# Bounds of the counting stage as 16-bit words without assertions, and in-degrees by one product per tile, in a four-layer graph network on one core

## The reference

```
x = layernorm(x + L0(x))   # attention, 4 heads: segment softmax of q[dst]*k[src], then a product, residual, norm
x = layernorm(x + L1(x))   # graph attention with loops, then a two-layer perceptron
x = layernorm(x + L2(x))   # h = x + segment_sum(relu(x[src]), dst); two dense layers; twice
x = layernorm(x + L3(x))   # graph convolution, then graph attention

def _gcn_conv(x, W, b, src, dst, n):      # first half of L3; src, dst with loops added
    xw = x @ W
    deg = jax.ops.segment_sum(jnp.ones(src.shape[0], x.dtype), dst, num_segments=n)
    dinv = jnp.where(deg > 0, jax.lax.rsqrt(deg), 0.0)
    norm = dinv[src] * dinv[dst]
    agg = jax.ops.segment_sum(xw[src] * norm[:, None], dst, num_segments=n)
    return agg + b
```

## Time and profile before

| | us |
|---|---|
| median of 3 runs | 3560.65 |
| lowest and highest | 3559.94 and 3570.57 |
| the profiled execution | 3559.3 |
| its span, first to last instruction | 3557.6 |
| PE busy | 3373.1 (95%) |
| DVE busy | 2598.0 (73%) |
| ACT busy | 2041.0 (57%) |

### The profile page before, as it was taken

The page is one execution under the profiler, slowest core; times in us unless marked ns, Lnnn a source line. Parts: engine busy times, 40 slices in busy tenths (PEclk is TensorE's granted clock), DMA queues, the critical chain, the costliest instruction groups (busy, mean ns, idle before and its releaser), DMA issues. The chain is left out here.

```text
span 3557.6 us, 67839 instructions
## 1 busy us (share of the span) xinstructions
PE 3373.1 (95%) x25864; PEld 2550.8 (72%) x25865; DVE 2598.0 (73%) x4774; ACT 2041.0 (57%) x3740; POOL 623.3 (18%) x602
## 2 busy tenths in 40 slices
PE   5999998999999999997999999999899999999999
PEld 3555555666676776766777777777688888878887
DVE  7888886666666666666999999999589443236665
ACT  2555556666666666665999899999311111115554
POOL 1000000111111111111235236666100100000000
PEclk9999999999999999998999999999999999999999
DMA  2555465233333333345333523333556555554341
GB/s 71 213 201 202 197 218 192 94 100 103 102 113 99 99 99 99 99 131 163 112 115 117 190 91 124 116 120 112 202 217 220 192 211 191 219 204 144 129 150 57
DMA packets 178028, 518.21 MB, mean 146 GB/s; under 512 B 54865, under 2 KB 140790, under 8 KB 144342
## 3 DMA queue, kind: packets, MB, share of 16 engines
q1 hardware_dynamic: 174822, 509.73, 41.2%
q10 hardware_dynamic: 1904, 3.81, 0.3%
q0 software_dynamic: 1024, 0.82, 0.1%
HBM read 353.04 MB, written 161.12 MB: 145 GB/s over the span
## 5 line engine op out<-in xcount | busy, mean ns | idle before, releaser
L1159 ACT ACTIVATE a_sm<-a_p_t 128x1024 f32<-128x1024 f32 (+1 forms) x800 | 669.6, 837 | 384.0 <-PE a_p_t L1095 378.2
L1095 PE MATMUL a_p_t<-ident,a_sm 128*128 128x128 f32 x5000 | 701.5, 280 | 35.4 <-ACT a_sm L1159 21.8
L1153 ACT ACTIVATE a_sm<-a_sm,a_negm 128x1024 f32<-128x1024 f32 (+2 forms) x600 | 702.8, 1171 | 49.8 <-DVE a_negm L1216 49.5
L1109 PE MATMUL a_p_o<-a_sm,a_v 128*64 128x128 f32 x10000 | 699.3, 278 | 19.0 <-ACT a_sumT L1166 17.7
L1095 PEld LDWEIGHTS a_p_t<-ident,a_sm 128*128 128x128 f32 x5000 | 559.1, 142 | 212.2 <-issue 193.0
L1109 PEld LDWEIGHTS a_p_o<-a_sm,a_v 128*64 128x64 f32 x10000 | 554.8, 137 | 196.6 <-issue 108.1
L1245 DVE CUSTOM_DVE_ANT_0 a_sm<-a_p_s,sh_rows 128x400 f32<-128x400 f32 x790 | 421.8, 571 | 345.6 <-PE a_p_s L1079 313.5
L1079 PE MATMUL a_p_s<-sh_wide,sh_q 64*128 64x400 f32 x1580 | 392.4, 550 | 12.0 <-DVE a_twice L1308 6.6
L1276 DVE CUSTOM_DVE_ANT_0 a_sm<-a_sm,sh_rows 128x3125 f32<-128x3125 f32 x100 | 348.5, 3485 | 1.3 <-issue 0.3
L1266 DVE SCALAR_TENSOR_TENSOR a_sm<-sh_wide,sh_al 128x3125 f32<-128x3125 f32 x100 | 346.9, 3469 | 3.5 <-PE a_p_o L1109 1.5
L693 ACT ACTIVATE sh_wide<-p_g 128x400 f32<-128x400 f32 x200 | 149.1, 901 | 246.5 <-PE p_g L608 246.5
(11 more groups left out here) (318 smaller groups left out, 4814.0 us busy)
## 6 DMA issues: line engine op xcount, KB each, us to landing
sh_rows<-d_full SPq DMA_DIRECT2D x67, 1600.0 KB, 7.0
sh_ct<-d_ct SPq DMA_DIRECT2D x50, 1600.0 KB, 6.8
d_ct<-sh_wide SPq DMA_DIRECT2D x25, 1600.0 KB, 5.3
d_full<-sh_rows SPq DMA_DIRECT2D x25, 1600.0 KB, 5.6
t_third<-d_ct SPq DMA_DIRECT2D x25, 1600.0 KB, 6.7
d_logs<-sh_rows SPq DMA_DIRECT2D x23, 1664.0 KB, 6.8
sh_rows<-d_logs SPq DMA_DIRECT2D x23, 1664.0 KB
t_mask<-d_full SPq DMA_DIRECT2D x8, 1600.0 KB, 6.8
```

The lines of the kernel that those rows point to most:

```text
L1095: m = nc.tensor.transpose(p_t[u % 2][:, i * P:(i + 1) * P], sm[buf][:, a * P:(a + 1) * P], ident[:, :])
L1109: m = nc.tensor.matmul(p_o[r:r + HD, 0:P], v[:, a, (p * heads + h) * HD:(p * heads + h + 1) * HD], sm[buf][:, a * P:(a + 1) * P], start=a ...
L1153: nc.scalar.activation(sm[buf][:, c], sm[buf][:, c], ACT.Exp, bias=negm[:, buf:buf + 1], accum_out=parts[:, buf, e:e + 1]).then_inc(s_prob, 1)
L1159: nc.scalar.activation(sm[buf][:, a_row[u] * P:a_row[u + 1] * P], p_t[u % 2][:, 0:turns[u] * P], ACT.Copy).then_inc(s_copy, 1)
```

## The change

`meta` becomes unsigned 16-bit. Both loads of it lose the run-time check of their bounds. The degree of a tile becomes one product: DVE adds `rest * real` into `by_low` after the reduction, and `s_by_low` counts two steps per tile.

```
-        meta = sb("meta", [1, NT, QPT * (2 + QUAD)], I32)
+        meta = sb("meta", [1, NT, QPT * (2 + QUAD)], U16)
...
                     _, said = nc.values_load_multi_w_load_instructions(
-                        meta[0:1, bass.ds(j, 1), :].rearrange("p n k -> p (n k)"), engines=[dve.engine], min_val=0, max_val=1 << 18)
+                        meta[0:1, bass.ds(j, 1), :].rearrange("p n k -> p (n k)"), engines=[dve.engine], min_val=0, max_val=(1 << 16) - 1, skip_runtime_bounds_check_because="loaded as unsigned 16-bit words")
...
                     _, said = nc.values_load_multi_w_load_instructions(
-                        meta[0:1, bass.ds(j, 1), 0:2 * QPT].rearrange("p n k -> p (n k)"), engines=[pe.engine], min_val=0, max_val=1 << 18)
+                        meta[0:1, bass.ds(j, 1), 0:2 * QPT].rearrange("p n k -> p (n k)"), engines=[pe.engine], min_val=0, max_val=(1 << 16) - 1, skip_runtime_bounds_check_because="loaded as unsigned 16-bit words")
...
-        pe.wait_ge(self.s_by_low, j + 1)
-        rest = self.ct[j % 3][:, (NT - 1) * P:NPAD].bitcast(FP32)
-        self.nc.tensor.matmul(self.p_deg[:, j:j + 1], rest, self.real[:, :], start=True, stop=False)
-        self.nc.tensor.matmul(self.p_deg[:, j:j + 1], self.by_low[j % 2][:, :], self.ones[:, :], start=False, stop=True).then_inc(self.s_deg_sum, 1)
+        pe.wait_ge(self.s_by_low, 2 * j + 2)
+        self.nc.tensor.matmul(self.p_deg[:, j:j + 1], self.by_low[j % 2][:, :], self.ones[:, :], start=True, stop=True).then_inc(self.s_deg_sum, 1)
...
-        self.nc.vector.tensor_reduce(self.by_low[j % 2][:, :], counts, AX.X, ALU.add).then_inc(self.s_by_low, 1)
+        rest = self.ct[j % 3][:, (NT - 1) * P:NPAD].bitcast(FP32)
+        by_low = self.by_low[j % 2][:, :]
+        self.nc.vector.tensor_reduce(by_low, counts, AX.X, ALU.add).then_inc(self.s_by_low, 1)
+        dve.wait_ge(self.s_by_low, 2 * j + 1)
+        self.nc.vector.scalar_tensor_tensor(by_low, rest, self.real[:, :], by_low, ALU.mult, ALU.add).then_inc(self.s_by_low, 1)
```

More of the change, by code:

```diff
@@ L10 @@
 I16 = mybir.dt.int16
+U16 = mybir.dt.uint16
 ALU = mybir.AluOpType
```

## The result

| | before | after |
|---|---|---|
| median of 4 runs each, lowest to highest (us) | 3563.13 (3559.94 to 3570.57) | 3524.54 (3521.93 to 3527.24) |
| ratio, 95% interval | | 0.9891 (0.9875 to 0.9906) |
| profiled execution, span | 3559.3, 3557.6 | 3527.2, 3525.5 |

The kernel became 1.1% faster, 38.6 us between the medians. The forecast was 1.5% (52 us, 3508), and the slow end of its range 3522. Lines of the counting stage have moved by one (537 is now 538, 545 is 546).

A forecast was written before the change was run, and what follows sets the result against it. DVE's sequencer bound the counting stage, with PE 0.6 us per tile behind; PE filled the last stage. Savings of 3.8, 3, 40 and 5.3 us made -52: 3508 us on the median's footing, range 3499 to 3522.

The forecast's parts named there:

- the price of the load: Counting stage, DVE's load of twelve table words per tile: stays 0.86 us with 16-bit words, at most twice that.
- The rest of the reckoning for DVE: Counting stage: DVE's 2.57 us gap before each tile's first key goes, leaving DVE 17.36 us per tile.
- DVE stays the bound: Rival, counting stage: dear 16-bit load or short sequencer lead leaves half the gap; period 18.6, 3521 us; chance 0.13.
- The assertions: Counting stage, DVE's sequencer: twelve pairs of register operation and assertion per tile go, worth 3.3 us (2.5 to 3.8).
- PE's floor: Counting stage: once DVE no longer starves it, PE binds at 18.0 us per tile.
- The rival of 18.4: Counting stage: PE also waits for ScalarE, so its floor is higher, period 18.4; 3517 us; chance 0.12.
- Terms of the stage: Counting stage savings: first tile -3.8 us, tiles 1 and 2 -3, tiles 3 to 24 -40.
- Part 2: Last stage's 25 sums: one degree product fewer each saves 5.5 us, less 0.2 in the first tile: -5.3.
- the margin: Last stage: DVE's fused operation stays hidden from PE, with 0.2 us left before the degree load, 0.1 before `t_h`.
- The dear fused operation: Rival, last stage: at 0.916 us PE waits for it every sum, turning -5.3 into +5; 3518 us; chance 0.04.
- Slower than before: Rival, counting stage: the 16-bit load takes over 4.2 us; 3600 us at 0.5 per word; chance 0.02.
- Transfers at nothing: Counting stage: transfers' share rises from 0.50 to 0.55 with the shorter tile; nothing charged.

The follow-up runs named there:

- e6: Changed kernel with PE loading all twelve words instead of four: PE's load 3.24 us instead of 0.99, period 18.70 us per tile instead of 18.67.
- e9: Changed kernel with DVE's load split into two of six 16-bit words, PE loading all twelve: 3546.45 us, ratio 0.9929 to the kernel before.
- e2: Changed kernel with the assertions kept on the 16-bit words: 3609.27 us, ratio 1.0128 to the kernel before.
- e1: Changed kernel with 32-bit words again, still without assertions, the number of earlier rounds masked: 3512.42 us, ratio 0.9858 to the kernel before.
- e10: e1 with the counting stage's stores of counts and logarithms cut to 128 columns per tile: period 18.10 us per tile.
- e11: e9 with the counting stage's stores of counts and logarithms cut to 128 columns per tile: period 18.13 us per tile instead of 20.23.
- e3: Kernel before with the new degree alone: 3560.44 us, ratio 0.9997 to the kernel before.
- e5: Changed kernel with a second, unread fused operation per degree: first degree to last 203.94 us instead of 199.15.
- e12: Changed kernel with the counting stage's stores of counts and logarithms cut to 128 columns per tile: period 18.59 us per tile instead of 18.67.
- e4: Changed kernel with each 16-bit word in a four-byte cell of its own: load 2.903 us, period 18.68 us per tile.
- e7: Changed kernel with signed 16-bit words, the number of earlier rounds masked: load 2.904 us, period 18.82 us per tile.

## Why the prediction was wrong

- **The failed step is the price of the load**: "I take 0.86: twelve words take 0.857 and four 0.333, about 0.066 each, which looks like a price per word, not per byte". Per word was right, on both engines (e6, e9). But two counts of one kind of word can't tell a price per word from one per 32-bit word. A 16-bit word costs 2.71 / 12 = 0.23 at an idle queue against 0.07, over three times as much, and the load of twelve takes 2.90 in the median. The upper bound, twice 0.86, was below that too; it was a guess without a row under it.
- **The rest of the reckoning for DVE held.** With 2.90 in place of 0.86 the same sum gives a gap of 2.57 - 3.3 + 2.04 = 1.31 and a period of 17.36 + 1.31 = 18.67. Measured: 1.34 and 18.67. So the price of the load is not one error among several in the loop, but the one that kept the bound at DVE.
- The Trainium skill, "Runtime: NRT & Kernel Launch", section "Instruction fetch mechanics", gives some 200 ns per register for such loads, of registers from HBM. I had set it aside because 32-bit words disagree (0.07). For 16-bit words the trace has 0.23 to 0.24, close to that figure, and the period it led to, 18.4, stood nearer to the 18.67 than my forecast. The nearness may be chance: the page speaks of another memory and says nothing of width. But it was a price for the same kind of instruction, and it should have set the upper bound of a form that no row showed.
- **The rival "DVE stays the bound"** came true with its mechanism (the 16-bit load is dear, about half the gap remains) and nearly its sizes: 18.6 and 3521, measured 18.67 and 3524.5. It had 0.13 of the chances, and the range ended with it, 2.5 us below the measured median.
- **The assertions**: 3.3 per tile forecast; by the periods of e2 and the changed kernel, which differ in them alone, 22.09 - 18.67 = 3.42. In e1, where nothing takes their place, DVE's gap is off the path and PE binds.
- **PE's floor**: 18.0 forecast, 18.11 in e1, 18.10 and 18.13 in e10 and e11. The rival of 18.4 is refuted.
- **Terms of the stage**: first tile -3.8 forecast, -1.2 measured (first product at 43.38 instead of 44.62; e1 -3.1); tiles 1 and 2 -3 forecast, -1.3 measured with tile 0 (e1 -1.9); tiles 3 to 24 -40 forecast, -26.4 measured (e1 -37.3). So of the 17.9 us missing in the stage, 13.4 are the narrow word, all of them back in e1, and 4.5 are missing in e1 too: 2.4 of them are the floor, 0.11 on 22 tiles, and what made the rest, mostly in the first three tiles, was not looked into.
- **Part 2**: -5.3 forecast; from the first degree to the last -5.3 in the changed kernel, -5.0 in e1 (199.47) and -3.9 in e3. The exact match is partly luck: one of the sums before took 8.67 where the others took 8.2. The steady gain is 0.21 per sum, as forecast. The fused operation was 0.34 in the forecast and is 0.352; the margin is as reckoned (e5). The dear fused operation (0.916) is refuted.
- **Slower than before** needed 4.2 us for the load. At 2.9 it kept 1.3 of distance; e2 shows what the same load does with the assertions beside it, 1.3% slower.
- **Transfers at nothing**: wrong in principle, though it cost little here. At shares of 0.13 and 0.25 the load is 0.2 and 0.4 us longer than at 0 (2.71), and e12, which didn't reach a share of 0, can't say what that is worth. The sign was in the maximum of 1139 ns in the earlier trace rows, which goes with a share of 0.75.

## What to carry to other kernels

An operand form that no row shows needs a range of its own: if the width of a word changes, the old price isn't a bound, and neither is twice the old price. Ask of each removal what had to change for it, and price that apart: the best version here drops the assertions and keeps the 32-bit words. And a load of registers on the engine that sets the pace belongs where its own queued work covers it and the transfer queues are quiet; moved into a burst of stores, six 16-bit words took up to 5.4 us.

## What the runs showed of the hardware

- A load of registers from SBUF, with the queues idle: twelve 32-bit words 0.85 us, twelve 16-bit words 2.71, six 16-bit words 1.39. On PE four take 0.33 and 0.99. Neither sign nor placement matters (2.90 in all three forms, medians of the changed kernel, e4 and e7).
- The same load under transfers: twelve 32-bit words 1.28 at a DMA share of 0.61 and 1.8 at 1.0; twelve 16-bit words 4.34 at 0.65; six 16-bit words 4.7 at 0.96. Each is a single load. The share alone doesn't set the length: six 16-bit words also took 1.38 at 1.03 (e9, tile 24).
- A run-time check of a loaded value is a register operation (0.183 us on DVE) and an assertion (0.023). Twelve of them were worth 3.42 us of the period where nothing hid them (e2 against the changed kernel) and 1.82 where PE's floor cut the gain off (e1 against before).
